# First batch's dt, b and gate without the split, early weights in two transfers, late weights' low halves one iteration later

## What is computed

```python
mod = (silu(c) @ wmod)                         # 16 x (6*256): sa, ca, ga, sb, cb, gb
h = layernorm(x) * (1 + ca) + sa
u, gate = split(h @ W_in.T)                    # 256 + 256 channels
b_t  = u @ W_state.T                           # 128 states
dt_t = minimum(softplus(u @ W_dt.T + b_dt), 10)
decay = exp(-dt_t * rate)
s_t = decay * s_(t-1) + (1 - decay) * b_t      # scan over the 512 tokens
z = (s @ W_C.T) * silu(gate) + h * D
x = x + ga * (z @ W_out.T)
h = layernorm(x) * (1 + cb) + sb
xk, xr = mixes of h and h shifted by one token
x = x + gb * sigmoid(xr @ W_r) * (square(relu(xk @ W_k)) @ W_v)
```

## Time and profile before

| | us |
|---|---|
| median of 3 runs | 377.53 |
| lowest and highest | 377.43, 378.26 |
| the profiled execution | 377.79 |
| its span in the trace | 375.9 |
| busy PE / PEld / DVE / ACT / POOL in the span | 359.1 / 276.4 / 302.0 / 308.8 / 265.6 |

### The profile page before, as it was taken

The page is one execution under the profiler, slowest core; times in us unless marked ns, Lnnn a source line. Parts: engine busy times, 40 slices in busy tenths (PEclk is TensorE's granted clock), DMA queues, the critical chain, the costliest instruction groups (busy, mean ns, idle before and its releaser), DMA issues.

```text
span 375.9 us, 5636 instructions
## 1 busy us (share of the span) xinstructions
PE 359.1 (96%) x1708; PEld 276.4 (74%) x1711; DVE 302.0 (80%) x637; ACT 308.8 (82%) x419; POOL 265.6 (71%) x274
## 2 busy tenths in 40 slices
PE   7999799999999999999999999999999999999773
PEld 4776477777778787777778777777778777776551
DVE  2788967988889797988989797988979787678452
ACT  4466779899898989899898989899898989886571
POOL 2073558969686878969686878969686876948552
PEclk9999999999999999999999999999999999999998
DMA  8931111130403131130403131130303030100011
GB/s 281 395 103 56 56 58 56 60 111 0 145 24 112 58 112 56 60 111 2 143 26 113 56 112 58 60 109 3 112 2 112 1 113 0 57 3 24 32 58 56
DMA packets 18607, 29.16 MB, mean 78 GB/s; under 512 B 1168, under 2 KB 9616, under 8 KB 18448
## 3 DMA queue, kind: packets, MB, share of 16 engines
q1 hardware_dynamic: 18144, 28.71, 22.1%
q10 hardware_dynamic: 432, 0.09, 0.1%
HBM read 20.40 MB, written 8.39 MB: 77 GB/s over the span
## 4 chain that ended last, share of the span: by engine, by line
POOL 47%; issue 39%; PE 5%; DVE 3%; ACT 2%; DMA 1%; POOLq 1%; DVEq 0%; SPq 0%; ACTq 0%
POOL xr_lo L730 11%; POOL z_lo L787 7%; POOL xk_lo L730 6%; POOL k_lo L730 6%; POOL h_lo L730 6%; POOL state_lo L777 5%; POOL rstd L740 3%; PE slot L220 2%; DMA w_in<-weights_in 1%; PE slot L234 1%; PE slot L347 1%; DVE stats L548 1%; POOL prev L771 1%; POOL spread L738 1%; POOL spread L737 1%
## 5 line engine op out<-in xcount | busy, mean ns | idle before, releaser
L766 POOL TENSOR_TENSOR rstd<-mv,half_neg 128x4 f32<-128x4 f32 x16 | 16.1, 1007 | 53.5 <-DVE mv L561 53.5
L435 ACT ACTIVATE prev<-slot,mod,mix_prev 128x512 f32<-128x512 f32 x64 | 46.3, 786 | 1.7 <-PE slot L227 1.7
L220 PE MATMUL slot<-h_hi,wf_hi 128*128 128x512 f32 x128 | 45.9, 399 | 0.4 <-ACT h_hi L461 0.4
L220 PE MATMUL slot<-h_hi,wf_lo 128*128 128x512 f32 x128 | 45.6, 397 | 0.0
L730 POOL TENSOR_TENSOR xk_lo<-xk,xk_hi 128x512 fp32r<-128x512 f32 x32 | 40.9, 1298 | 6.6 <-ACT xk_hi L446 5.8
L787 POOL TENSOR_TENSOR z_lo<-z,z_hi 128x512 fp32r<-128x512 f32 x28 | 36.2, 1294 | 12.0 <-ACT z_hi L442 7.9
L730 POOL TENSOR_TENSOR k_lo<-k_act,k_hi 128x512 fp32r<-128x512 f32 x32 | 40.7, 1293 | 4.9 <-ACT k_act L516 4.9
L730 POOL TENSOR_TENSOR xr_lo<-xr,xr_hi 128x512 fp32r<-128x512 f32 x32 | 42.5, 1331 | 0.0
L730 POOL TENSOR_TENSOR h_lo<-h,h_hi 128x512 fp32r<-128x512 f32 x30 | 38.3, 1302 | 3.1 <-ACT h_hi L461 3.1
L227 PE MATMUL slot<-ident,xn 128*128 128x128 f32 x256 | 35.9, 274 | 2.8 <-DVE xn L585 2.1
L227 PEld LDWEIGHTS slot<-ident,xn 128*128 128x128 f32 x256 | 29.5, 141 | 11.4 <-issue 4.9
(11 more groups left out here) (121 smaller groups left out, 1002.9 us busy)
## 6 DMA issues: line engine op xcount, KB each, us to landing
x_tok<-x_tok_in SPq DMA_DIRECT2D x16, 512.0 KB, 3.5
x_ch<-x_ch_in SPq DMA_DIRECT2D x16, 512.0 KB, 3.7
x_out<-wmod SPq DMA_DIRECT2D x15, 512.0 KB, 3.0
wmod<-wmod_in SPq DMA_DIRECT2D x1, 1024.0 KB, 10.0
w_in<-weights_in SPq DMA_DIRECT2D x1, 1024.0 KB, 11.5
w_in<-weights_in SPq DMA_DIRECT2D x1, 768.0 KB, 5.5
wmod<-wmod_in SPq DMA_DIRECT2D x1, 512.0 KB, 6.4
x_out<-wmod SPq DMA_DIRECT2D x2, 256.0 KB, 2.2
```

The source lines that it names most:

```text
L220: ins = nc.tensor.matmul(out, w[:, c, at + d * P:at + (d + 1) * P], x[:, c, :], start=first, stop=last)
L435: return nc.scalar.activation(prev[:, mix, i, 1:T + 1], ps_n[:, i, :], ACT.Identity, bias=mod_at(SHIFT2 + i, k), scale=mix_prev[:, mix, i, ...
L766: nc.gpsimd.tensor_tensor(rstd2[:, c % 2], mv2[:, c % 2, 1, :], half_neg[:], ALU.pow).then_inc(rstd2_ok, 1)
```

## The change

The dt, b and gate products of batch 0 are made in plain float32 from `h`, `w_front` and `w_early`; `h_hi` and `h_lo` of batch 0 are no longer made. ACT writes the first channel half of `h` first, with a semaphore of its own (`h0_ok`). The early weights are loaded in two pieces (the part for the folded weights, then the gate's after the first part of `wmod`); the rest of `wmod` is loaded before the tokens of batch 2. PE multiplies zeros 10 times instead of 13 and 4 times instead of 11, and does three columns of the rest of the modulation before `ps_y` instead of two, without zeros between them. The statistics of batch 2 are moved from step 0 to step 1 on DVE, and its mean and variance behind `z`. ACT applies batch 1's layernorm after silu. POOL makes the low halves of the K, R and V weights in step 2 right after `h_lo` of batch 1, instead of at the end of step 1.

```diff
--- before.py
+++ after.py
@@ -179,13 +180,15 @@
             load_tokens(0)
-            sp.dma_start(w_in[:, 0:CH * 3 * C], w_d[:, 0:CH * 3 * C]).then_inc(s_w, 16)
+            w_early_d = w_d[:, 0:CH * 3 * C].rearrange("p (c n) -> p c n", c=CH)
+            sp.dma_start(w_early[:, :, 0:GATE], w_early_d[:, :, 0:GATE]).then_inc(s_w, 16)
             wmod_cols = wmod_d.rearrange("(c p) n -> p c n", p=P)
             sp.dma_start(wmod[:, :, 0:2 * C], wmod_cols[:, :, 0:2 * C]).then_inc(s_wmod, 16)
+            sp.dma_start(w_early[:, :, GATE:], w_early_d[:, :, GATE:]).then_inc(s_wgate, 16)
             load_tokens(1)
             sp.dma_start(w_y, w_d[:, CH * 7 * C:]).then_inc(s_wy, 16)
+            sp.dma_start(wmod[:, :, 2 * C:], wmod_cols[:, :, 2 * C:]).then_inc(s_wmod2, 16)
             load_tokens(2)
-            sp.dma_start(wmod[:, :, 2 * C:], wmod_cols[:, :, 2 * C:]).then_inc(s_wmod2, 16)
             sp.dma_start(w_in[:, CH * 3 * C:CH * 7 * C], w_d[:, CH * 3 * C:CH * 7 * C]).then_inc(s_wl, 16)
...
@@ -245,7 +248,7 @@
             pe.wait_ge(zeros_ok, 1)
-            keep_warm(slot[0][:, 0, :], 13)
+            keep_warm(slot[0][:, 0, :], 10)
             pe.wait_ge(s_w, 16)
...
@@ -277,26 +280,40 @@
                     half(o_out, wl_hi, OUT, z_lo, 1, last=True).then_inc(o_ps, 1)
-                if live(b):
-                    if b == 0:
+                if b == 0:
+                    pe.wait_ge(front_ok, 1)
+                    pe.wait_ge(h0_ok, 1)
+                    half(dt_out, w_front, 0, h[:, 0], 0, first=True)
+                    pe.wait_ge(h_ok, 1)
+                    half(dt_out, w_front, 0, h[:, 0], 1, last=True).then_inc(dt_ps, 1)
+                    half(b_out, w_front, NS, h[:, 0], 0, first=True)
+                    half(b_out, w_front, NS, h[:, 0], 1, last=True).then_inc(b_ps, 1)
+                    pe.wait_ge(s_wgate, 16)
+                    half(g_out, w_early, GATE, h[:, 0], 0, first=True)
+                    half(g_out, w_early, GATE, h[:, 0], 1, last=True).then_inc(g_ps, 1)
+                    pe.wait_ge(s_wmod2, 16)
+                    for j in range(3):
+                        modulation(4 + j, 1, slot[2][:, 1, j * NB:])
+                elif live(b):
+                    if b == 1:
                         pe.wait_ge(wsplit_lo, 2)
-                    pe.wait_ge(hhi_ok, b + 1)
+                    pe.wait_ge(hhi_ok, b)
                     for i in range(CH):
...
                     half(k_out, wl_hi, MIX_K, xk_lo, 0)
-                if live(b):
+                if live(b) and b > 0:
                     for i in range(CH):
...
                     half(k_out, wl_hi, MIX_K, xk_lo, 1, last=True).then_inc(k_ps, 1)
-                if live(b):
-                    pe.wait_ge(hlo_ok[0], b + 1)
-                    pe.wait_ge(hlo_ok[1], b + 1)
+                if live(b) and b > 0:
+                    pe.wait_ge(hlo_ok[0], b)
+                    pe.wait_ge(hlo_ok[1], b)
                     half(dt_out, wf_hi, 0, h_lo, 0)
...
@@ -325,14 +342,11 @@
                     half(r_out, wl_lo, MIX_R, xr_hi, 1)
-                if live(b):
+                if live(b) and b > 0:
                     half(g_out, wf_hi, 2 * NS, h_lo, 0)
                     half(g_out, wf_hi, 2 * NS, h_lo, 1, last=True).then_inc(g_ps, 1)
+                if live(b):
                     if b == 0:
-                        pe.wait_ge(s_wmod2, 16)
-                        for j in range(2):
-                            modulation(4 + j, 1, slot[2][:, 1, j * NB:])
-                            keep_warm(slot[1][:, 0, :], 1)
                         pe.wait_ge(s_wy, 16)
...
@@ -347,7 +361,7 @@
                     if b == 0:
-                        for j in range(2, 8):
+                        for j in range(3, 8):
                             last = modulation(4 + j, 1, slot[2][:, 1, j * NB:])
...
@@ -390,7 +404,7 @@
                 if a == 0:
-                    keep_warm(slot[3][:, 0, :], 11)
+                    keep_warm(slot[3][:, 0, :], 4)
                 if live(d):
...
@@ -431,6 +445,14 @@
 
+            def ln1_apply(k):
+                act.wait_ge(shift1_ok, k + 1)
+                before(act, t1_ps, k)
+                for t in range(TT // 2):
+                    last = nc.scalar.activation(xn1[:, t, :], x_tok[:, k % 3, t, :], ACT.Identity,
+                                                bias=shift1[:, k % 2, t:t + 1], scale=rstd1[:, k % 2, t:t + 1])
+                last.then_inc(xn1a_ok, 1)
+
             def previous(mix, i, k):
...
@@ -450,14 +472,15 @@
                     before(act, z_ok[1], b - 1)
-                    nc.scalar.activation(h[:, b % 2, 1, :], ps_h[:, 1, :], ACT.Identity, bias=mod_at(SHIFT1 + 1, b), scale=mod_at(SCALE1 + 1, b))
+                    nc.scalar.activation(h[:, b % 2, 0, :], ps_h[:, 0, :], ACT.Identity, bias=mod_at(SHIFT1, b), scale=mod_at(SCALE1, b)).then_inc(h0_ok, 1)
                 if live(d):
...
                 if live(b):
-                    nc.scalar.activation(h[:, b % 2, 0, :], ps_h[:, 0, :], ACT.Identity, bias=mod_at(SHIFT1, b), scale=mod_at(SCALE1, b)).then_inc(h_ok, 1)
+                    nc.scalar.activation(h[:, b % 2, 1, :], ps_h[:, 1, :], ACT.Identity, bias=mod_at(SHIFT1 + 1, b), scale=mod_at(SCALE1 + 1, b)).then_inc(h_ok, 1)
+                if live(b) and b > 0:
                     act.wait_ge(h_ok, b + 1)
-                    before(act, g_ps, b)
+                    act.wait_ge(g_ps, b)
                     nc.scalar.copy(h_hi[:], h[:, b % 2]).then_inc(hhi_ok, 1)
...
@@ -485,13 +508,8 @@
                     nc.scalar.preload_act_table_set("silu_and_others")
-                if live(a):
-                    act.wait_ge(shift1_ok, a + 1)
-                    before(act, t1_ps, a)
-                    for t in range(TT // 2):
-                        last = nc.scalar.activation(xn1[:, t, :], x_tok[:, a % 3, t, :], ACT.Identity,
-                                                    bias=shift1[:, a % 2, t:t + 1], scale=rstd1[:, a % 2, t:t + 1])
-                    last.then_inc(xn1a_ok, 1)
+                if live(a) and a != 1:
+                    ln1_apply(a)
                 if split(b):
...
@@ -504,6 +522,8 @@
                     nc.scalar.activation(silu[:], ps_gate[:], ACT.Silu).then_inc(silu_ok, 1)
+                if a == 1:
+                    ln1_apply(a)
                 if b == 0:
...
@@ -623,6 +643,7 @@
             nc.vector.tensor_copy(wf_hi[:, :, 0:2 * NS], w_front[:])
+            dve.wait_ge(s_wgate, 16)
             nc.vector.tensor_copy(wf_hi[:, :, 2 * NS:], w_early[:, :, GATE:GATE + C]).then_inc(wsplit_hi, 1)
...
@@ -633,9 +654,6 @@
             nc.vector.tensor_scalar(rate[:, 0:1], rate[:, 0:1], -1.0, None, ALU.mult).then_inc(rate_ok, 1)
-            dve.wait_ge(hhi_ok, 1)
-            for i in range(CH):
-                nc.vector.tensor_tensor(h_lo[:, i], h[:, 0, i], h_hi[:, i].bitcast(F32), ALU.subtract).then_inc(hlo_ok[i], 1)
             ln1_stats(1)
...
@@ -648,8 +666,8 @@
                 if b == 0:
-                    ln1_mean_variance(2)
                     ln1_apply(1)
+                    ln1_stats(2)
                 if live(c):
...
@@ -668,6 +686,7 @@
                 if b == 0:
+                    ln1_mean_variance(2)
                     rest_of_modulation()
...
@@ -711,7 +730,6 @@
                     ln1_mean_variance(1)
-                    ln1_stats(2)
                 if live(b):
...
@@ -756,7 +774,12 @@
                     for i in range(CH):
-                        low_part(h_lo[:, i], h[:, b % 2, i], h_hi[:, i], hhi_ok, g_ps, hlo_ok[i], b)
+                        pool.wait_ge(hhi_ok, b)
+                        pool.wait_ge(g_ps, b)
+                        nc.gpsimd.tensor_tensor(h_lo[:, i], h[:, b % 2, i], h_hi[:, i].bitcast(F32), ALU.subtract).then_inc(hlo_ok[i], 1)
+                if b == 1:
+                    for n, at in ((1, MIX_K), (2, MIX_R), (3, MIX_V)):
+                        weight_low_part(n, at)
                 if live(d):
...
@@ -785,9 +808,6 @@
                         nc.gpsimd.tensor_tensor(z_lo[:, i], z[:, i], z_hi[:, i].bitcast(F32), ALU.subtract).then_inc(zlo_ok[i], 1)
-                if b == 0:
-                    for n, at in ((1, MIX_K), (2, MIX_R), (3, MIX_V)):
-                        weight_low_part(n, at)
                 if b == 1:
...
                     pool.wait_ge(wy_hi_ok, 1)
```

More of the change, by code:

```diff
@@ L122, in adaln_block @@
         ps_gate, ps_n, ps_k = slot[3], slot[3], slot[3]
-        s_w, s_wl, s_wy = sem("w_in"), sem("w_late_in"), sem("w_y_in")
+        s_w, s_wgate, s_wl, s_wy = sem("w_in"), sem("w_gate_in"), sem("w_late_in"), sem("w_y_in")
         s_wmod, s_wmod2, s_cols, s_c, s_id = sem("wmod_first_in"), sem("wmod_rest_in"), sem("cols_in"), sem("c_in"), sem("ident_in")
@@ L139, in adaln_block @@
         t2_ps, t3_ps, k_ps, r_ps, v_ps = sem("t2_ps"), sem("t3_ps"), sem("k_ps"), sem("r_ps"), sem("v_ps")
```

(2 more changed lines are left out.)

## The result

| | us |
|---|---|
| median of the changed kernel, 5 runs | 380.49 |
| lowest and highest | 378.88, 381.24 |
| median of the kernel before, same number | 377.53 |
| ratio, 95% interval | 1.0073, 1.0051 to 1.0095 |
| the profiled execution and its span | 381.06, 379.3 |

The kernel became slower by 2.96 us. The forecast was 378.0 with a range up to 378.7; the time lies outside it.

A forecast was written before the change was run, and what follows sets the result against it. PE was taken as the bound once full near 44 us, with DVE the bound from 30.85 to 38.94. The terms -1.35 + 1.85 = +0.50 us on the median 377.53 gave 378.0; range 376.1 to 378.7.

The forecast's parts named there:

- Part 4: POOL's low halves behind `h_lo` of batch 1 hold DVE's apply (plus 1.01 us) and clip: plus 1.85 us in all.
- The one doubt: At DVE's clip: if it gets through ahead of V, -1.35 + 1.01 = -0.34 us, time 377.2; chance 0.19.
- Part 2: Batch 0's products in float32: state 2.8 us earlier, PE the bound, `ps_y` 1.35 us earlier, 0.92 without part 1.
- part 1: Loads and warmers before the loop: transposes start at 9.88, gain 0.43 us, 0 if the smaller transfer lands no earlier.
- so is `ps_y` (PE idle 1.37 there): After the clip of batch 2: the drive at 36.93, and `ps_y` with it, is later by the whole 1.85 us.
- Rival (d): At the start, fewer zeros leave PE's clock at 1.2 GHz: near 1.5 us worse than forecast, 379.5; chance 0.06.
- A shift of the start is a shift of the end, one for one: Once PE is full, near 44 us, any shift carries unchanged to the end; the period stays 21.2 us.

The follow-up runs named there:

- the low halves first: Changed kernel with POOL's K, R and V low halves in step 1 ahead of the scale of batch 2: 376.8 us median, ratio 0.9967 to the kernel before.
- both sets of zeros: Changed kernel with 13 multiplications of zeros ahead of `ps_y` of batch 1 and 8 + 8 in the last steps: 378.73 us median, ratio 1.0025.

## Why the prediction was wrong

- **Part 4, the collision**: right in mechanism and in size. The forecast had 1.01 us for the apply and 0.84 for the clip; measured 0.97 and 1.04. The one doubt, whether V holds the clip, was resolved as forecast, in every profile in which V stood there.
- **Part 2, batch 0 in float32**: right in mechanism. PE took the scan's place as the bound; the three columns ended as `ps_y` started. The gain at `x1` was 1.02 us instead of 1.35. The missing 0.33 is of **part 1**: the transposes started at 10.18 and not 9.88, since the fold took 2.50 us instead of 1.99; why is not shown. Profiles of kernels with the same start differ here: with the low halves back at the end of step 1 they show the forecast's own numbers, transposes at 9.85 and `x1` at 29.49; with the low halves first the fold took 1.99 us, PE waited 0.52 us for `wmod` (8.62), and the start was 10.43, the `x1` 30.08. So the gain at `x1` is between 0.77 and 1.36 us from one execution to the next. The forecast had the tokens as the next bound and did not ask whether `wmod` might be late.
- **The step that failed**: "so is `ps_y` (PE idle 1.37 there)". The forecast moved the drive and let PE wait, and put the wait itself at nothing. It did not add up that PE would come earlier by the gain and the state later by the cost, which made 3.39 us of 1.37, nor ask what PE's clock does then. PE did its next work at half clock: 0.8 us lost in one profile, 1.9 in another. Rival (d) had the clock, but at the zeros of the start only. It was the experiments with zeros that showed the wait as the cause, since filling it kept the clock at 1.00 with the drive as late as in the changed kernel (37.81 against 37.92). The POOL move alone, in a kernel with all its zeros, gives the same fall.
- **"A shift of the start is a shift of the end, one for one"** held from 59 to 335 us (0.11 us) and failed behind it: in the profiled execution the clock fell at 362 us and 1.5 us went. From the last scan's start to the end of the span only this profile (44.5 us) and that of the POOL move alone (43.87) are longer; nine other profiles of variants have 42.9 to 43.1. How often it happens in executions without a profile stays open, and so does its cause, since the wait of 2.2 us is the same in the kernel before. The medians split the two stretches roughly: zeros in the wait took 1.48 us off, zeros at the end 0.31, both 1.76, with spreads of about 2 us in the first two. Most of the loss is thus in the wait at 36 us.
- **Range**: its upper end was the collision's cost without a term for the clock. 378.73 with the clock kept up lies 0.03 us above its upper end. Of its distance to the forecast of 378.0, 0.49 us is the gain too small and the clip held longer (the drive 0.99 us later and not 0.50); what lies beyond 378.73 is the clock.

## What to carry to other kernels

In this kernel a block of GpSimd work cost nothing where VectorE had no float32 `tensor_scalar` from SBUF to SBUF to do (0.40 us alone, 1.45 beside it), and 3.9 us where it had two such lines on the critical path. Look for a line whose shortest and longest times differ by a whole GpSimd instruction, and for the place in GpSimd's list where it waits anyway. When a change lengthens a wait of TensorE, add up how long it becomes from both sides (TensorE earlier, its operand later), price the work behind it at half clock too, and look whether other executions of the same kernel spread more than before. An undo of one part isn't the old kernel: what the block queues behind may have moved.

## What the runs showed of the hardware

- With the same start and PE waiting 3.4 us, one execution kept its clock until 41 us and another lost it at 39 us; a wait of 2.2 us in the last steps was followed by full clock in one kernel and by 0.54 in another. The Trainium skill (TensorE: Matmul & The Clock Gate, Part 1) has half rate as the default that activity lifts, and that the same kernel shows different counts of slow multiplications from run to run; this case agrees in so far as the changed kernel spreads from 378.88 to 381.24 us, and with both sets of zeros six of seven executions lie from 378.66 to 378.93.
- A fall of the clock isn't always a loss. In the kernel with the low halves first it was at 0.56 and 0.58 from 354 to 358 us, and yet it was 42.94 us from the last scan's start to the end of the span, against 43.0 in the kernel before, and the runs stayed within 0.5 us.
